# Attention's heads 1 to 6 written out in place of a loop, and a new order for its last stretch

## The reference

```
q = einsum('btd,ndh->btnh', x, q_kernel)      # 16 query heads of 128
k, v = einsum('bsd,ckdh->cbskh', x, kv_kernel)  # 8 key/value heads
q = rope(rms_norm(q)); k = rope(rms_norm(k))
mask = (j <= i) & (i - j < 256)
probs = softmax(q k^T * scale + mask)
enc = probs v;  y = einsum('btnh,nhd->btd', enc, out_kernel)
x = x + layernorm(y)
```

## Time and profile before

| | us |
|---|---|
| median of 3 runs (2064.32 to 2067.83) | 2066.57 |
| the profiled execution | 2065.59 |
| its span | 2063.8 |
| scan, gated network and head 0, to the loop | 513 |
| heads 1 to 6 (the loop; PE's six branches at its end from 626.8 to 1199.3) | 686 |
| last stretch of attention and norm | 184 |
| experts | 681 |

### The profile page before, as it was taken

The page is one execution under the profiler, slowest core; times in us unless marked ns, Lnnn a source line. Parts: engine busy times, 40 slices in busy tenths (PEclk is TensorE's granted clock), DMA queues, the critical chain, the costliest instruction groups (busy, mean ns, idle before and its releaser), DMA issues. The chain is left out here.

```text
span 2063.8 us, 33157 instructions
## 1 busy us (share of the span) xinstructions
PE 1962.0 (95%) x10142; PEld 1660.0 (80%) x10142; DVE 1483.1 (72%) x3410; ACT 1200.1 (58%) x2978; POOL 797.2 (39%) x1200
## 2 busy tenths in 40 slices
PE   7999999999999999999999989969999999999996
PEld 6677777778888888888888878858788898888875
DVE  7788555787777777777777767975377787775665
ACT  6752222576666666666666656764376777674342
POOL 4441000685555555555555546861600000000452
PEclk9999999999999999999999999989999999999998
DMA  7343010217000000000000000132799998884563
GB/s 262 125 136 137 16 47 21 92 62 230 21 12 22 10 22 10 21 11 1 22 10 21 31 1 8 61 106 95 257 334 310 326 319 315 309 304 145 197 206 114
DMA packets 82657, 245.03 MB, mean 119 GB/s; under 512 B 10800, under 2 KB 11440, under 8 KB 80592
## 3 DMA queue, kind: packets, MB, share of 16 engines
q1 hardware_dynamic: 77376, 226.46, 32.1%
q0 software_dynamic: 5120, 16.78, 2.3%
HBM read 207.81 MB, written 45.61 MB: 123 GB/s over the span
## 5 line engine op out<-in xcount | busy, mean ns | idle before, releaser
L307 PE MATMUL l_xp<-att_w_hi,xT_hi 128*128 128x512 f32 x512 | 210.1, 410 | 4.4 <-ACT att_qkv L2414 4.4
L307 PE MATMUL l_xp<-att_w_hi,xT_lo 128*128 128x512 f32 x512 | 203.0, 397 | 0.0
L307 PE MATMUL l_xp<-att_w_lo,xT_hi 128*128 128x512 f32 x512 | 203.0, 397 | 0.0
L946 POOL TENSOR_SCALAR att_pr<-att_pr,rec_ri 128x384 f32<-128x384 f32 (+2 forms) x256 | 141.1, 563 | 125.5 <-DVE rec_ri L1614 125.5
L2443 ACT ACTIVATE att_pr<-att_pr,rec_nb,rec_r 128x384 f32<-128x384 f32 (+2 forms) x256 | 168.6, 661 | 35.4 <-DVE rec_nb L1585 34.5
L3874 POOL DMA_INDIRECT y<-moe_rows,moe_slotA x16 | 16.2, 1010 | 415.8 <-DMA moe_rows<-moe_lo_f 412.6
L1581 DVE CUSTOM_DVE_ANT_0 att_pr<-l_dd,att_mask 128x384 f32<-128x384 f32 (+2 forms) x256 | 119.2, 502 | 78.7 <-PE l_dd L307 60.9
L950 POOL TENSOR_TENSOR att_rot<-att_rot,att_rot 128x384 f32<-128x384 f32 x128 | 129.7, 1014 | 109.1 <-DVE att_rot L1608 109.1
L2414 ACT ACTIVATE att_qkv<-l_xp 128x512 f32<-128x512 f32 x128 | 76.5, 598 | 142.3 <-PE l_xp L307 110.0
L1619 DVE TENSOR_TENSOR att_pT_lo<-l_out,att_pT_hi 128x768 fp32r<-128x768 f32 (+2 forms) x128 | 108.9, 850 | 23.2 <-ACT att_pT_hi L2436 22.9
L2436 ACT ACTIVATE att_pT_hi<-l_out 128x768 fp32r<-128x768 f32 (+2 forms) x128 | 92.3, 721 | 48.3 <-PE l_t L307 24.4
(11 more groups left out here) (325 smaller groups left out, 6575.6 us busy)
## 6 DMA issues: line engine op xcount, KB each, us to landing
y<-in_moe_rt SPq DMA_DIRECT2D x59, 704.0 KB, 6.7
y<-in_moe_rt SPq DMA_DIRECT2D x39, 768.0 KB, 6.7
moe_sraw_gu<-in_moe_sgu SPq DMA_DIRECT2D x44, 512.0 KB, 3.7
moe_sraw_d<-in_moe_sd SPq DMA_DIRECT2D x44, 256.0 KB, 4.5
moe_xs<-in_zeros SPq DMA_DIRECT2D x39, 256.0 KB, 7.3
moe_lo_f<-moe_xs SPq DMA_DIRECT2D x39, 256.0 KB, 7.0
moe_rows<-moe_lo_f SPq DMA_DIRECT2D x39, 256.0 KB, 6.8
att_raw_w<-in_qkv_w SPq DMA_DIRECT2D x8, 1024.0 KB, 4.8
```

The lines of the kernel that those rows point to most:

```text
L307: mm = pe.matmul(out, lhsT, rhs, start=(i == 0), stop=(i == len(terms) - 1))
L946: pool.tensor_scalar(p, p, ri[:, j % 2, g:g + 1], 1.0, ALU.mult, ALU.mult).then_inc(sa("p"), 1)
```

## The change

Two things. The loops over heads 1 to 6 become Python loops on the four engines, so that the six bodies stand in the program one behind the other, with constants in place of registers; their order within a head is the same. And the last stretch has the same steps in another order on all four engines. SP's program is unchanged.

```diff
@@ GpSimd; the same at L1822 (DVE), L2646 (ACT), L3385 (PE) @@
-            with pool.Fori(1, KVH - 1) as k:
+            for k in range(1, KVH - 1):
...
@@ PE, behind the loop @@
             pe.wait_ge(sa("cleared"), 1)
+            turn_p(10, 106)
+            project(6, 15, 111)
             project_out(6, 8, 104)
             scores(12, 108)
-            turn_p(10, 106)
             turn(13, 109)
-            project_out(6, 9, 105)
             turn_p(11, 107)
             weigh_v(10, 106)
-            project(6, 15, 111)
+            project_out(6, 9, 105)
+            turn(14, 110)
             scores(13, 109)
...
@@ PE, the end @@
             project_out(7, 14, 126)
             weigh_v(15, 127)
+            last_turn(1, 0)
             last_turn(1, 1)
+            project_out(7, 15, 127)
             last_turn(1, 2)
-            project_out(7, 15, 127)
             last_turn(1, 3)
...
@@ DVE, where the norm begins @@
+            split_e(1, 113)
+            rope(6, 118)
+            split_p(2, 114)
+            inverse(4, 116)
             sum_out(0, 112, False)
-            rope(5, 117)
             norm.y_stats(dve, 0, (0,))
...
@@ POOL, the end @@
             norm.x_rstd_shift(pool, 3, (0,))
+            norm.y_rstd_shift(pool, 3, (3,))
             norm.x_add(pool, 3, (2,), True)
-            norm.y_rstd_shift(pool, 3, (3,))
             norm.x_rstd_shift(pool, 3, (1,))
```

More of the change, by code:

```diff
@@ L1821, in _ @@
             dve.wait_ge(sa("y_zero"), 1)
-            with dve.Fori(1, KVH - 1) as k:
+            for k in range(1, KVH - 1):
                 row_max(12, NT * k - 4)
@@ L2645, in _ @@
             qkv_out(15, 15)
-            with act.Fori(1, KVH - 1) as k:
+            for k in range(1, KVH - 1):
                 split_w_part(k, 0)
@@ L2804, in _ @@
             split_qk(2, 114)
-            split_p(0, 112)
-            split_e(15, 111)
+            split_e(14, 110)
+            split_p(15, 111)
+            exps(1, 113)
             qkv_out(4, 116)
@@ L2891, in _ @@
+            split_qk(11, 123)
+            split_e(8, 120)
+            split_p(9, 121)
+            norm.y_norm(act, 1, (3,))
             qkv_out(14, 126)
-            norm.y_norm(act, 2, (0,))
             squares(14, 126)
             split_v(14, 126)
+            split_qk(12, 124)
+            split_e(9, 121)
+            split_p(10, 122)
+            exps(11, 123)
+            norm.y_norm(act, 2, (0,))
+            qkv_out(15, 127)
+            norm.x_norm_act(act, 0, (3,))
+            squares(15, 127)
@@ L2919, in _ @@
-            exps(15, 127)
-            split_p(14, 126)
-            norm.x_norm_act(act, 2, (1,))
-            norm.hi(act, 0, (1,))
+            split_qk(15, 127)
+            norm.x_norm_act(act, 1, (2,))
+            exps(14, 126)
+            split_e(12, 124)
+            norm.hi(act, 0, (0,))
+            norm.y_norm(act, 2, (2,))
+            norm.hi(act, 0, (1,))
+            split_p(13, 125)
+            norm.y_norm(act, 2, (3,))
+            exps(15, 127)
+            norm.x_norm_act(act, 1, (3,))
@@ L3384, in _ @@
             weigh_v(9, 9)
-            with pe.Fori(1, KVH - 1) as k:
+            for k in range(1, KVH - 1):
                 turn_p(10, NT * k - 6)
@@ L3516, in _ @@
+            project(7, 4, 116)
+            project_out(6, 13, 109)
+            scores(2, 114)
+            turn_p(0, 112)
+            turn(3, 115)
+            project(7, 5, 117)
+            weigh_v(15, 111)
+            scores(3, 115)
             project_out(6, 14, 110)
-            turn(2, 114)
-            turn_p(0, 112)
-            weigh_v(15, 111)
-            project(7, 4, 116)
+            turn_p(1, 113)
+            turn(4, 116)
+            weigh_v(0, 112)
             project_out(6, 15, 111)
-            scores(2, 114)
```

581 lines of the change are left out of this document (276 added, 305 removed).

## The result

| | before | after |
|---|---|---|
| median, us | 2065.99 (4 runs, 2064.32 to 2067.83) | 2043.24 (4 runs, 2038.54 to 2046.68) |
| the profiled execution | 2065.59 | 2038.54 |
| its span | 2063.8 | 2036.6 |

The ratio is 0.9892 with an interval of 0.988 to 0.9905: 22.8 us faster. The forecast was 2045.5. The profiled execution of after is the shortest of its four, 4.7 us under their median, so its trace holds some microseconds that do not belong to the change.

What follows compares the result with a forecast made beforehand. PE's work and waits until the barrier that ends attention were taken as the bound. Branches 9.1, last stretch 12 and tail 0 sum to 21.1 us, 2066.57 to 2045.5 us; range 2038.5 to 2054.

Steps and rivals of the forecast that it cites:

- What bounds the kernel: Attention: PE's work plus its waits set each head; finishing sooner moves the router's load behind the barrier by as much.
- Part A: Heads 2 to 6: written out, they are entered like head 1, saving five taken branches; 9.1 us, ends 4.6 to 12.
- The price of streaming: Heads 2 to 6: bringing in PE's straight code, about 30 instruction blocks on q8, costs 0.
- The rival of code that comes too late: Heads 2 to 6: PE loses 1.8 us at each of 30 blocks, 54 us, giving 2099 us; chance 0.03.
- Part B: Joint behind the loop and the stretch after it: the new order removes PE's waits and lower clock; 12 us, ends 6 to 17.
- PE's way of the sum: Joint behind the loop: PE's waits fall from 9.05 to 0.5 us, plus 3.9 us of lower clock; together 12.4 us.
- clock term: Joint behind the loop: with the idle gone, PE's two periods at the lower clock go too; 3.9 us.
- DVE's way: Head 7: first `sum_out` at 1263.7, the last 91.2 us later at 1354.9, which is 12.5 us sooner.
- The circle: Joint behind the loop: ACT waits 10.05 us for tile 111's late projection, DVE waits for ACT, PE for DVE.
- DVE eats the gain: Last stretch: the norms bunched on DVE cut the stretch's gain to 6 us, giving 2051.5 us; chance 0.17.
- Part C: Tail of the norm, from last `sum_out` to last `lo`, 13.4 us: no change, 0, ends -1.5 and +1.5.
- The sum: Whole kernel: 9.1 + 12 + 0 = 21.1 us saved, from a median of 2066.57 to 2045.5 us.

Runs made afterwards that it cites:

- dve_act_out: The changed kernel with PE's and POOL's loops put back, only DVE and ACT written out; 2042.24 us of 2065.31, ratio 0.9887.
- the probe: The changed kernel with dummy loops of 40, 100, 200 and 400 one-column writes, four turns each, at DVE's start; not compared in time.
- pe_joint: The kernel before with only PE's first 13 steps behind the loop in the new order; 2054.16 us of 2065.89, ratio 0.994.
- stretch_only: The changed kernel with the four loops put back, keeping the new order of the last stretch; 2055.07 us of 2065.31, ratio 0.9948.
- unroll_only: The kernel before with the four loops written out, the last stretch in its old order; 2052.42 us of 2065.31, ratio 0.9936.
- proj_first: The kernel before with one PE step moved: tile 111's projection first behind the loop; 2058.63 us of 2065.31, ratio 0.9965.
- small: The kernel before with DVE's and ACT's loops written out and PE's first 13 steps behind the loop in the new order; 2040.98 us of 2066.21.
- pe_pairs: The changed kernel with only PE's heads 1 to 6 as a loop of three turns of two heads; 2050.88 us of 2065.89, ratio 0.9925.

## Why the prediction was right, point by point

**What bounds the kernel.** Right: PE's work in the heads and the barrier behind them. All that attention gained reached the router's load, at 1358.08. It had been put at 1362; the difference is the 1.2 us before head 1, the 3.1 us of part A's shortfall, and little else.

**Part A, forecast 9.1 us, measured 12.2.** The mechanism held (DVE and ACT start late behind a branch, PE does not), the term was too small. The step that failed is "Written out, heads 2 to 6 are entered as head 1 is". Head 1 is entered from head 0. Its last steps stand in the order of a body's end (12 on POOL, 13 on PE, 19 on DVE, 23 on ACT), but for one that only head 0 has: POOL's `clear_y`, a memset of 3.10 us among them. Behind it `weigh` of tile 12 starts 5.15 us after tile 15's projection, in head 2 only 3.82, and PE waits 0.5 us for it in head 1 (the change; before):

```profile
509.42 3.10 POOL L955 MEMSET y<- 128x3584 f32 x1
...
520.70 0.88 PE L3217 MATMUL l_out<-ident,att_pr 128*128 128x128 f32 x6 [0.54 <-POOL att_pr L946]
```

No run leaves this memset out, so it is the likeliest cause of the wait and not a shown one; in any case the wait belongs to the entry from head 0 and not to a head. Heads 2 to 6 are entered from a body's own end, and there PE waits for nothing: 112.05, which is the upper end that was named (112.07, 12 us in all). With a branch the entry cost 114.49 - 112.05 = 2.44 and not 1.83. What was said of single engines was less complete than it sounded: the text followed DVE's late `row_max` to PE's wait, but ACT's late start alone leads to 1.9 of the 2.4 us, and so does DVE's alone. Who had written out only DVE on the strength of rows 5 would have had a fifth of part A's gain.

**The price of streaming, forecast 0.** Right, by `dve_act_out` against the change. The rival of code that comes too late (2099 us) needed 0.7 us at each of 30 blocks; with and without the blocks the heads differ by at most 0.02 us. The Trainium skill (Runtime: NRT & Kernel Launch, Instruction fetch mechanics) says that a crossing into the next block is mostly hidden, and that a taken branch whose target is no longer in the window stalls for a fetch. The runs agree with both: PE with one head a body loops free, with two it stalls 2.7 to 3.1 us. Straight code at full load shows no price, and only between instructions as short as the probe's is there a gap of about 0.33 us; that this gap is the crossing is inferred from its even distance of 128 instructions.

**Part B, forecast 12, measured 12.2** (the remainder of 14.6, as said above; 12.5 in `pe_joint`, 10.6 in `stretch_only`). PE's way of the sum held: idle 9.05 to about 0.5, and the lower clock gone. But its clock term, 3.9 us, is less sure than it looks: the same wait of 2.92 us was followed by 3.8 us of lower clock before, 6.5 in `unroll_only` and none in `proj_first`, which is 0 to 3 us for one wait. DVE's way had the first `sum_out` at 1263.7 and 91.2 us behind it; in the trace after these are 91.1, and the first `sum_out` is as forecast once what came sooner ahead of it is taken off (1263.7 - 12.2 for part A - 1.2 for the start = 1250.3; it was 1250.67). But `pe_joint` and `small` show that this way proved nothing on its own: with the old order on DVE the first `sum_out` comes 56.1 us behind tile 111's projection (after: 63.4), the last 98.2 us behind that (after: 91.1), and both ways end at 154.3 to 154.5 us. The count of steps ahead of a landmark moves the landmark and not the end. The circle was the right reason for most of it, but not for all: the projection's place is 8.2 of the 12.2 us, the lower clock's 3.9 among them, and the other 4 came with `project_out` of tile 105 behind `turn_p` and `weigh_v`, where it no longer waits for `sum_out`. The prediction had these 2.92 us in its sum, without a cause of their own.

**DVE eats the gain (0.17).** It did not, though the waits between the two `sum_out`s did grow, PE's from 4.8 to 7.2 us and DVE's from 2.7 to 3.6, inside the 8 that were named as the limit. (The 5.4 of the prediction are of a longer stretch, and leave out two waits of 0.4.)

**Part C, forecast 0, measured -0.45** (13.8 us and not 13.4), within its ends. The old tail in `small` took 13.4 again.

**The sum.** 21.1 forecast, 23.9 in the traces and 22.8 in the medians. The median stands 2.3 us below the forecast, of which 0.6 come from the median of before, which is now 2065.99 and not 2066.57. Part A, 3.1 us too small, is the one term that was off by more than 0.5. The 1.1 us between traces and medians can't be read: the interval of the ratio is 19.6 to 24.8 us.

## What to carry to other kernels

A loop's price stands where its engines start again, not in the loop's own instructions: look for "issue" waits right behind the branch on every engine, and follow each to the engine that bounds; where two of them lead to the same wait, removing one brings almost nothing. Write out the loops of the engines that show such a wait, and leave the others as they are; a longer body is not a cheaper one, since past the size that an engine keeps it pays at every turn. And don't count on the lower clock behind a wait as on the wait itself: the same wait brought it in some kernels and not in others. Where an order written by hand meets the end of a loop, go on with the loop's own order there for as long as its tiles are open: 13 steps on the engine that bounds were worth as much as a new plan for all four.

## What the runs showed of the hardware

- A taken branch on DVE costs 0.30 to 0.46 us for bodies of 40 to 200 operations and 2.87 to 3.17 us for 400. In the kernel DVE pays 2.5 to 2.8 us with 272 operations in the body (346 instructions with those of its sequencer), ACT 2.0 to 2.3 with 260 (396), and POOL nothing with 201 instructions in all.
- On PE a body of one head (643 matmuls and 642 weight loads by the trace, some 1400 instructions in all) is free. A body of two heads costs 2.7 to 3.1 us of issue wait at each branch, and then 1.5 us more at the lower clock, 4.5 us in all.
- Straight code is free for PE at full load (112.03 of 112.06 us busy in a head while six blocks come), but dense one-column operations on DVE show a gap of 0.33 us every 128.
- The lower clock behind a wait is not certain: behind the same wait of 2.92 us the granted clock was 0.56 over 3.80 us (before), 0.53 over 6.48 (`unroll_only`) and 1.00 (`proj_first`); behind one of 2.2 us it was 0.52 over 3.40 us in `stretch_only` and 1.00 in the change.
- A branch's wait and the lower clock behind it are separate costs. The second falls where the engine is busy, so no list of waits has it: of `pe_pairs`' 9.0 us in the intervals, the waits list shows 5.5.
